# Convolution and involution over 32 images: patches for the 7x7 taps stored in DRAM plane by plane

## The chip, the core and the metric

The kernel runs on one core of a Trainium2 chip. The metric is the device time of one execution in microseconds; the number for a kernel is the median of its runs. The engines of the core are TensorE (PE; its weight loads are shown as PEld), VectorE (DVE), ScalarE (ACT), GpSimd (POOL) and SyncE (SP). SP and ACT both issue DMAs, each on a queue of its own, and the 16 DMA engines of the core serve both queues.

## What is computed

The input is `x` of 32 images x 64 channels x 56 x 56, in float32. Two residual steps follow each other, each on a group norm with 32 groups of two channels. This is the reference, cut:

```python
# step 1: binary 3x3 convolution
xb, wb = jnp.sign(_gn(x)), jnp.sign(weight)
x = x + conv(xb, wb, padding=1) * scale
# step 2: involution, 7x7 taps, 16 groups of 4 channels
v = _gn(x)
r = relu(batchnorm(w_r @ v + b_reduce))          # 64 -> 16 channels
ker = (w_s @ r + b_span)                         # 16 -> 49 * 16 channels, one 7x7 kernel per pixel and group
for ki in range(7):
    for kj in range(7):
        out = out + vpad[:, :, :, ki:ki + H, kj:kj + W] * ker[:, :, ki * 7 + kj][:, :, None]
x = x + out
```

## The kernel before

Two images make a **pair**, whose 2 x 64 channels are the 128 partitions; there are 16 pairs. For each pair the kernel makes the convolution on PE and adds it on DVE (`chunks`), takes the statistics (`variance`, `root`, `affine`), and normalizes (`normalize`, ACT) into `xn`. Since the span weights are the same for every pixel, the involution is reordered: PE multiplies shifted patches of `v` with the span weights (`taps`), DVE multiplies the result with `r` (`product`, L792), POOL folds two halves (L365), and PE sums over the 16 channels of `r` (`sums`).

**Patches.** A patch matrix has taps and positions on the partitions and pixels on the free dimension. It stands in two stacks of 128 rows, `X1` (`patches`, three buffers) and `X2` (`patches2`, two buffers), each fp16. They are filled out of DRAM: PE transposes `xn` (`transposes`), ACT copies the result in fp16, the high part (`high`, L404), DVE takes the rest, the low part (`low`, L783), and SP writes both to `D` in DRAM (`parts_out`, L270), four pieces k of 256 KB in each of two DMAs a pair. ACT's `high` of piece k waits until piece k-2 has been written, since the two share a buffer.

A pair's image is cut into seven **strips** (I call them s = 0 to 6). A stack row group of 16 rows is a **plane**: a part (high or low) with a vertical offset. For every strip SP loads the eight planes of `X1` with eight DMAs of 16 rows (`first_stack`, L287), and two low planes of `X2` with two DMAs (`second_stack`, L295). Their rows are 32 to 95 in steps of 4, and 0 to 31 and 96 to 127 in steps of 2. The other five planes of `X2` are planes that `X1` has too; ACT copies them in SBUF, 96 rows by 1792 columns in each of four instructions (`copy_high`, L432). The selection matrices of `constants()` place each tap's weights on the rows where its plane stands.

**Order.** Every engine runs a program written out by hand. A strip has eight units n; unit n of all 56 of a pair is `taps` on PE, `product` on DVE, a fold on POOL. The tables at the top of the file (L75 to L86) say behind which unit of the current pair each piece of work for the next pair stands: the convolution at units 11 to 17 (strips 1 and 2), the statistics at 18 to 21 (strip 2), the transposes with `high` and `low` at 28, 30, 34, 36 (strips 3 and 4), the reduction with `relu` at 37 and 38 (strip 4). Of a strip's eight ACT steps, the four copies for the next strip stand at steps 0, 1, 4 and 5, `gather` of the strip before (osb from PSUM, then a DMA to `sums_dram`) at step 3, and `rows` at step 7, which waits for that DMA to land and then loads it into `U`. `arrange` (L454) reorders `U` at units 13 and 46.

SP's program for strip e is: the second stack of strip e+1 (it waits until strip e-1 has left PE), the first stack of strip e+2, in strip 2 the store of the pair before, in strip 3 pieces 0 and 1 of the next pair's parts and the load of x for the pair after, in strip 4 pieces 2 and 3 and `spread`, 16 small DMAs that distribute `r` (L305). PE begins a strip when both its stacks are in and its copies are made (L564 to L566):

```python
                if n % GP == 0:
                    pe.wait_ge(first_in[e % 3], FIRSTLOAD * (e // 3 + 1))
                    pe.wait_ge(second_in[e % 2], SECONDLOAD * (e // 2 + 1))
                    pe.wait_ge(copied, JX * (e + 1))
```

## Time and profile before

| what | value |
|---|---|
| time, three runs | median 1971.62 us (1965.9 to 1975.86) |
| the profiled execution's own time | 1978.51 us |
| its span in the trace | 1976.6 us |
| mean granted TensorE clock | 0.922 |
| busy share: PE, DVE, ACT, POOL | 82%, 70%, 53%, 51% |
| DMA, moved | 410.7 MB, mean 208 GB/s |

The profile page and the trace are of one execution. A busy share is an average over the whole span. The views used below are the page, the table of waits (which engine stood idle before which line, and what it was that ended the idle time), tables by windows of time, timelines of one engine, and the list of DMA issues with the median time from issue to landing. In a row, `L432` is line 432 of the kernel, `SPq` and `ACTq` are DMA issues on those queues, and a bracket at the end gives the idle time before it and what ended it.

### The profile page before, as it was taken

How to read it: one execution, taken by the hardware profiler on the slowest of the kernel's cores; microseconds unless marked ns; L12 is line 12 of the kernel's file. 1: busy time of each engine (PE TensorE's matmuls, PEld its weight loads, DVE VectorE, ACT ScalarE, POOL GpSimd, SP SyncE). 2: the span in 40 equal slices, each digit the busy share in tenths (PEclk: the TensorE clock that was granted, in tenths of full speed). 3: DMA queues.
4: the chain of work that ended last, by engine and by line, in shares of the span. 5: the costliest groups of instructions: out<-in, count | busy, mean ns of one | idle time of the engine just before them, and what ended most of it. 6: DMA issues, size and time to landing. Idle time of an engine off the chain costs nothing.

```text
span 1976.6 us, 39046 instructions
## 1 busy us (share of the span) xinstructions
PE 1621.0 (82%) x15072; PEld 730.2 (37%) x15072; DVE 1378.6 (70%) x1699; ACT 1052.8 (53%) x758; POOL 1015.0 (51%) x904
## 2 busy tenths in 40 slices
PE   3488897978889797896978878798887988889885
PEld 1233443434333343343433334333333433334332
DVE  5476776858768685776867767586776767768674
ACT  2255555545655554555545655465555545655562
POOL 1145555554645555455554645555455554645673
PEclk8799998999999998998989989898989999989997
DMA  4679899797998969899798998979799797998993
GB/s 106 158 168 237 185 238 224 199 233 172 245 216 217 236 173 239 186 244 215 188 240 181 250 215 205 230 183 247 175 240 225 187 250 180 248 215 205 227 243 85
DMA packets 215178, 410.70 MB, mean 208 GB/s; under 512 B 87406, under 2 KB 134815, under 8 KB 210847
## 3 DMA queue, kind: packets, MB, share of 16 engines
q1 hardware_dynamic: 139728, 356.81, 74.2%
q10 hardware_dynamic: 75264, 51.39, 10.1%
q8 instruction: 119, 1.95, 0.5%
q14 instruction: 67, 0.55, 0.1%
HBM read 310.30 MB, written 84.93 MB: 200 GB/s over the span
## 4 chain that ended last, share of the span: by engine, by line
POOL 46%; issue 42%; SPq 4%; DMA 2%; DVE 2%; PE 2%; ACT 1%; POOLq 1%; ACTq 0%; DVEq 0%
POOL folded L365 46%; SPq L305 2%; DMA patches<-parts_dram 1%; SPq L287 1%; PE ybank L571 1%; DMA back<-consts_dram 1%; POOLq L364 0%; SPq L257 0%; ACT patches L432 0%; DVE prod L792 0%; SPq L295 0%; PE ybank L541 0%; DMA parts_dram<-parts 0%; DVE parts L783 0%; SPq L270 0%
## 5 line engine op out<-in xcount | busy, mean ns | idle before, releaser
L365 POOL TENSOR_TENSOR folded<-prod 128x448 f32<-128x448 f32 x896 | 1009.3, 1139 | 941.3 <-DVE prod L792 940.0
L792 DVE TENSOR_TENSOR prod<-ybank,relu 128x896 f32<-128x896 f32 x896 | 961.1, 1088 | 406.9 <-PE ybank L571 333.4
L571 PE MATMUL ybank<-patches,wspan 128*64 128x448 f16 x7168 | 863.7, 382 | 240.2 <-DMA patches<-parts_dram 110.4
L432 ACT ACTIVATE patches<-patches 96x1792 f16<-96x1792 f16 x448 | 736.8, 1689 | 589.8 <-DMA patches<-parts_dram 306.9
L571 PEld LDWEIGHTS ybank<-patches,wspan 128*64 128x64 f16 x7168 | 396.3, 116 | 757.6 <-issue 416.1
L512 PE MATMUL ybank<-sgn,convw 128*128 128x448 bf16 x1008 | 205.6, 357 | 24.5 <-ACT sgn L385 20.1
L589 PE MATMUL obank<-folded,esum 128*32 128x448 f32 x1792 | 214.8, 551 | 1.5 <-POOL folded L365 1.5
L582 PE MATMUL obank<-patches,wbias 128*32 128x448 f16 x3584 | 197.8, 364 | 0.0
L512 PEld LDWEIGHTS ybank<-sgn,convw 128*128 128x128 bf16 x1008 | 93.4, 97 | 137.8 <-issue 33.5
L582 PEld LDWEIGHTS obank<-patches,wbias 128*32 128x32 f16 x3584 | 87.4, 99 | 105.2 <-issue 52.7
L783 DVE TENSOR_TENSOR parts<-ybank,parts 128x1024 f16<-128x1024 f32 x64 | 78.5, 1226 | 60.5 <-ACT parts L404 60.5
L750 DVE SCALAR_TENSOR_TENSOR xs<-ybank,scale,xs 128x896 f32<-128x896 f32 x64 | 66.0, 1032 | 73.7 <-PE ybank L512 73.6
L404 ACT ACTIVATE parts<-ybank 128x1024 f16<-128x1024 f32 x64 | 65.3, 1020 | 68.1 <-PE ybank L541 64.5
L603 PE MATMUL ybank<-back,blocks 128*128 128x128 f32 (+1 forms) x448 | 62.2, 284 | 44.2 <-DVE prod L792 36.0
L541 PE MATMUL ybank<-ident,xn 128*128 128x128 f32 x512 | 74.3, 293 | 20.9 <-DVE parts L783 20.1
L420 ACT ACTIVATE osb<-obank,alpha 128x448 f32<-128x448 f32 x112 | 69.3, 619 | 29.7 <-PE obank L589 29.7
L603 PEld LDWEIGHTS ybank<-back,blocks 128*128 128x128 f32 (+1 forms) x448 | 48.2, 153 | 77.7 <-DVE prod L792 52.2
L541 PEld LDWEIGHTS ybank<-ident,xn 128*128 128x128 f32 x512 | 59.4, 148 | 44.4 <-DVE parts L783 25.5
L454 ACT ACTIVATE blocks<-rows 128x1792 f32<-128x1792 f32 (+1 forms) x32 | 54.1, 1690 | 40.0 <-DMA relu<-blocks 31.9
L754 DVE BATCH_NORM_STATS2 bn<-xs 128x6 f32<-128x448 f32 x112 | 70.2, 627 | 3.9
L804 DVE TENSOR_TENSOR xs<-ybank,xs 128x1024 f32<-128x1024 f32 (+1 forms) x64 | 61.8, 966 | 12.8 <-PE ybank L603 12.7
L734 DVE TENSOR_REDUCE rowsums<-xs 128x14 f32<-128x784 f32 x64 | 61.1, 959 | 12.5 <-DMA xs<-x_dram 12.5
(90 smaller groups left out, 380.0 us busy)
## 6 DMA issues: line engine op xcount, KB each, us to landing
patches<-parts_dram SPq DMA_DIRECT2D x1120, 224.0 KB, 7.0
parts_dram<-parts SPq DMA_DIRECT2D x128, 256.0 KB, 7.7
xs<-x_dram SPq DMA_DIRECT2D x128, 196.0 KB, 5.0
sums_dram<-osb ACTq DMA_DIRECT2D x112, 224.0 KB, 6.2
rows<-sums_dram ACTq DMA_DIRECT2D x112, 224.0 KB, 6.6
out_dram<-xs SPq DMA_DIRECT2D x128, 196.0 KB, 3.7
relu<-blocks SPq DMA_DIRECT2D x256, 49.0 KB
patches<-gb_dram SPq DMA_DIRECT2D x1, 784.0 KB
```

What stands on the lines that cost most here:

```text
L365: pool.tensor_tensor(folded[:, u % 8, :], prod[:, u % 2, 0, :], prod[:, u % 2, 1, :], ALU.add).then_inc(fold_done, 1)
L420: act.activation(osb[:], Obank[e % 2][:, 0:N], ACT.Copy, scale=alpha[:]).then_inc(o_read, 1)
L432: act.activation(X2[0:COPIED_ROWS, e % 2, at], X1[0:COPIED_ROWS, e % 3, at], ACT.Copy).then_inc(copied, 1)
L512: mm = pe.matmul(bank("conv", p, k)[:, i, 0:CW], convw[:, tap, :], sgn[:, CR * row + dh:CR * row + dh + CR, dw:dw + W], start=(tap == 0), ...
L541: mm = pe.transpose(bank("t", p, k)[:, y, 128 * h:128 * h + 128], xn[:, COLS * cy:COLS * cy + COLS], ident[:])
L571: mm = pe.matmul(bank("unit", p, n)[64 * t:64 * t + 64, h, 0:N], wspan[:, stack, g, h, :], of_group(e, stack, g), start=(stack == 0), stop ...
L582: pe.matmul(Obank[e % 2][32 * t:32 * t + 32, 0:N], wbias[:, stack, g, :], of_group(e, stack, g), start=(stack == 0 and i == 0), stop=False)
L589: mm = pe.matmul(Obank[e % 2][32 * (gp // 2):32 * (gp // 2) + 32, 0:N], esum[:, 16 - 16 * (gp % 2):48 - 16 * (gp % 2)], folded[:, 4 * half ...
L603: mm = pe.transpose(bank("out", p, k)[:, i, rows * n:rows * (n + 1)], V[0:rows, by].rearrange("m b g c -> m (b g c)"), back[0:rows, group, ...
L754: link(dve.bn_stats(bn[:, row, :], at[:, i, :]))
L783: dve.tensor_tensor(at(1), bank("t", p, k)[:], at(0), ALU.subtract).then_inc(low_done, 1)
L792: dve.tensor_tensor(prod[:, u % 2].rearrange("m h (n c) -> m h n c", c=GC), bank("unit", p, n)[:, :, 0:N].rearrange("m h (n c) -> m h n c" ...
```

## The change

- `D` is replaced by two DRAM tensors. `D0` holds for each of 128 source rows the eight planes of `X1`, each in a run of 2048 elements that is already shifted by the plane's offset. `D1` holds the two low planes of `X2`. A part that several planes need is written once for each: `parts_out` issues ten DMAs for piece 0 and six for each of the others, where it issued two, and writes 10 planes where there were 4 half images (5.0 MB a pair where it was 2.1 MB).
- The first stack of a strip is one DMA of 128 partitions, on SP. The rows of the stack are now 8 r + q, for row r of plane q.
- ACT copies all 128 rows of the first stack to the second, at steps 0, 1, 2 and 3 of a strip. It then waits for its own copies and issues two DMAs, on its own queue, that load the two low planes over rows 3, 11, ... and 7, 15, ... of `X2`. `gather` moves from step 3 to step 4.
- The load and the store of a pair's x are one DMA of 128 partitions each, where they were eight of 16.

```diff
-COPIED_ROWS, COPIED_PLANES = 96, 5
+PLANES = (((0, 0), (0, 2), (0, 4), (1, 1), (0, 1), (0, 3), (1, 0), (1, 2)),
+          ((0, 0), (0, 2), (0, 4), (1, 3), (0, 1), (0, 3), None, (1, 4)))
+Q = 8
+
+LOADED = (3, 7)
...
-XLOAD, STORE = 16 * 8, 16 * 8
-FIRSTLOAD, SECONDLOAD = 16 * 8, 16 * 2
+XLOAD, STORE = 16, 16
+FIRSTLOAD, SECONDLOAD = 16, 16 * 2
 COPY = JY * 128
-DWRITE = 16 * 2
+DWRITE = (16 * 10, 16 * 6)
...
-SUMS_B, BIAS, SUMS_A, ROWS_AT = 3, 6, 7, 7
-
-COPY_AT = {0: 0, 1: 1, 4: 2, 5: 3}
+SUMS_B, GATHER, BIAS, SUMS_A, ROWS_AT = 3, 4, 6, 7, 7
+
+COPY_AT = {0: 0, 1: 1, 2: 2, 3: 3}
...
             def load(p):
-                for rows in ROWS16:
-                    sp.dma_start(xs[rows, p % 3, :], xv[p][rows]).then_inc(x_loaded, 16)
+                sp.dma_start(xs[:, p % 3, :], xv[p]).then_inc(x_loaded, 16)
...
-                for l in range(2):
-                    sp.dma_start(D[p % 2, l].rearrange("m (y h n) -> m y h n", y=2, h=4)[:, :, k, :],
-                                 Ev[:, l, k % 2]).then_inc(d_written[k], 16)
+                b = p % 2
+
+                def run(dram, planes, q, l, y, shift, many):
+
+                    src = Ev[:, l, k % 2, y]
+                    if k == 0:
+                        for i in range(many):
+                            cut = BLOCK * (shift + i)
+                            sp.dma_start(dram[b, :, q + i, 0:4 * BLOCK - cut], src[:, cut:]).then_inc(d_written[k], 16)
+                        return
+                    dst = bass.AP(tensor=dram.tensor, offset=(128 * b * planes + q) * RUN + BLOCK * (4 * k - shift),
+                                  ap=[[planes * RUN, 128], [RUN - BLOCK, many], [1, 4 * BLOCK]])
+                    sp.dma_start(dst, src.unsqueeze(1).broadcast_to((128, many, 4 * BLOCK))).then_inc(d_written[k], 16)
+
+                run(D0, Q, 0, 0, 0, 0, 3)
+                run(D0, Q, 4, 0, 1, 0, 2)
+                run(D0, Q, 6, 1, 0, 0, 2)
+                run(D0, Q, 3, 1, 1, 0, 1)
+                run(D1, 2, 0, 1, 1, 1, 1)
+                run(D1, 2, 1, 1, 0, 2, 1)
...
-                for l, a, row, step in PLANES[0]:
-                    sp.dma_start(X1[row:row + 15 * step + 1:step, e % 3, :],
-                                 plane(e, l, a)).then_inc(first_in[e % 3], 16)
...
+                sp.dma_start(X1[:, e % 3, :].rearrange("p (j n) -> p j n", j=JX), stack(D0, e)).then_inc(first_in[e % 3], 16)
...
-                act.activation(X2[0:COPIED_ROWS, e % 2, at], X1[0:COPIED_ROWS, e % 3, at],
-                               ACT.Copy).then_inc(copied, 1)
+                act.activation(X2[:, e % 2, at], X1[:, e % 3, at], ACT.Copy).then_inc(copied, 1)
+
+            def second_stack(e):
+
+                act.wait_ge(copied, JX * (e + 1))
+                if e >= 2:
+                    act.wait_ge(second_in[e % 2], SECONDLOAD * (e // 2))
+                p = e // E
+                for i, q in enumerate(LOADED):
+                    src = bass.AP(tensor=D1.tensor, offset=(2 * (128 * (p % 2) + 4 * JX * (e % E)) + i) * RUN,
+                                  ap=[[2 * RUN, 16], [8 * RUN, JX], [1, JY * 128]])
+                    act.dma_start(X2[q:128:Q, e % 2, :].rearrange("p (j n) -> p j n", j=JX), src).then_inc(second_in[e % 2], 16)
```

The first place to look at is ACT, from `normalize` in strip 2 through strip 3 to strip 4. A row is an instruction with what it writes and reads; `parts` is `high`, `osb` and `sums_dram` are `gather`, `patches2` are the copies. Before:

```order
L396 ACTIVATE xn<-xs,small 128x28x56 x2
L445 DMA rows<-sums_dram 32x16x112
L432 ACTIVATE patches2<-patches 96x1792 x2
L420 ACTIVATE osb<-obank0,alpha 128x448
L424 DMA sums_dram<-osb 128x448
L404 ACTIVATE parts<-ybank2 128x1024
L432 ACTIVATE patches2<-patches 96x1792 x2
L404 ACTIVATE parts<-ybank2 128x1024
L445 DMA rows<-sums_dram 32x16x112
L432 ACTIVATE patches2<-patches 96x1792 x2
L404 ACTIVATE parts<-ybank1 128x1024
```

The same stretch of ACT in the changed kernel:

```order
L399 ACTIVATE xn<-xs,small 128x28x56 x2
L458 DMA rows<-sums_dram 32x16x112
L435 ACTIVATE patches2<-patches 128x1792 x4
L446 DMA patches2<-planes2_dram 16x4x1792 x2
L407 ACTIVATE parts<-ybank2 128x1024
L423 ACTIVATE osb<-obank0,alpha 128x448
L427 DMA sums_dram<-osb 128x448
L407 ACTIVATE parts<-ybank2 128x1024
L458 DMA rows<-sums_dram 32x16x112
L435 ACTIVATE patches2<-patches 128x1792 x2
L407 ACTIVATE parts<-ybank1 128x1024
```

In strip 3 all four copies and the two DMAs of the second stack now stand ahead of the first `high`, where two copies and `gather` stood; in strip 4 `high` still stands behind two copies.

The second place is SP from strip 3 to strip 5, before: `parts_dram` are the pieces, `xs` the load of x, `relu` is `spread`.

```order
L270 DMA parts_dram<-parts 256x1x512 x4
L257 DMA xs<-x_dram 16x3136 x8
L295 DMA patches<-parts_dram 16x4x1792 x2
L287 DMA patches<-parts_dram 16x4x1792 x8
L270 DMA parts_dram<-parts 256x1x512 x4
L305 DMA relu<-blocks 16x1x784 x16
L295 DMA patches<-parts_dram 16x4x1792 x2
L287 DMA patches<-parts_dram 16x4x1792 x8
```

The same place in the changed kernel, from the end of piece 1 of the next pair's parts:

```order
L281 DMA planes_dram<-parts 128x512 x3
L257 DMA xs<-x_dram 128x3136
L302 DMA patches<-planes_dram 128x4x1792
L281 DMA planes_dram<-parts 128x3x512
L281 DMA planes_dram<-parts 128x2x512 x2
L281 DMA planes_dram<-parts 128x512 x3
L281 DMA planes_dram<-parts 128x3x512
L281 DMA planes_dram<-parts 128x2x512 x2
L281 DMA planes_dram<-parts 128x512 x3
L311 DMA relu<-blocks 16x1x784 x16
L302 DMA patches<-planes_dram 128x4x1792 x5
```

The second stack no longer stands behind the 16 DMAs of `spread`; the first stack still does, and pieces 2 and 3 are 12 issues ahead of `spread` where they were four.

## Rows read from the trace of the kernel before

**Rows 1.** The page: busy time of the engines, and the two DMA queues.

```profile
PE 1621.0 (82%) x15072; PEld 730.2 (37%) x15072; DVE 1378.6 (70%) x1699; ACT 1052.8 (53%) x758; POOL 1015.0 (51%) x904
...
q1 hardware_dynamic: 139728, 356.81, 74.2%
q10 hardware_dynamic: 75264, 51.39, 10.1%
```

**Rows 2.** The table of waits: us in total, times, longest us.

```profile
ACT patches L432 <- DMA patches<-parts_dram: 306.9, 45, 13.1
...
PE ybank L571 <- DMA patches<-parts_dram: 110.4, 15, 9.1
PE ybank L571 <- ACT patches L432: 91.5, 29, 20.0
```

**Rows 3.** Windows, DVE's products alone: stretch, us, DVE busy, PEclk, DMA share, GB/s.

```profile
923.50:937.40 13.90, 8.64 (x9) 0.94 0.96 214
937.40:958.70 21.30, 8.51 (x9) 1.00 0.55 135
958.70:975.30 16.60, 8.59 (x9) 1.00 0.82 206
975.30:988.20 12.90, 8.61 (x10) 1.00 0.99 252
988.20:1007.10 18.90, 8.63 (x10) 0.91 1.05 262
1007.10:1024.90 17.80, 8.61 (x9) 0.89 0.82 226
1024.90:1041.40 16.50, 8.60 (x8) 0.91 1.04 232
```

**Rows 4.** Windows: us, busy PE PEld DVE ACT POOL, PEclk, DMA share, GB/s.

```profile
2.50:3.10 0.60, 0.00 (x0) 0.00 (x0) 0.00 (x0) 0.00 (x0) 0.60 (x1) 1.00 0.92 363
...
4.00:11.00 7.00, 0.00 (x0) 0.00 (x0) 0.00 (x0) 1.35 (x2) 2.22 (x3) 1.00 0.99 216
...
57.60:68.00 10.40, 5.59 (x46) 1.96 (x44) 3.67 (x3) 4.67 (x5) 0.00 (x0) 0.97 0.60 202
...
77.40:79.00 1.60, 0.00 (x0) 0.00 (x0) 0.00 (x0) 0.32 (x1) 0.00 (x0) 0.50 1.01 201
...
988.20:1007.10 18.90, 16.37 (x158) 6.23 (x158) 10.92 (x12) 11.12 (x9) 9.88 (x9) 0.91 1.05 262
```

**Rows 5.** Timeline of SP's issues: start, us, line, what is moved, count.

```profile
7.29 0.36 SPq L316 DMA_DIRECT2D patches<-gb_dram  x1
...
1001.18 2.55 SPq L270 DMA_DIRECT2D parts_dram<-parts  x4
1005.52 12.81 SPq L305 DMA_DIRECT2D relu<-blocks  x16
1018.43 1.26 SPq L295 DMA_DIRECT2D patches<-parts_dram  x2
```

**Rows 6.** Timeline of PE, the first units of strip 6 of this pair.

```profile
1023.15 4.67 PE L571 MATMUL ybank<-patches,wspan 128*64 128x448 f16 x24 [7.09 <-DMA patches<-parts_dram]
```

**Rows 7.** Timeline of ACT in strips 2 and 3 of this pair.

```profile
966.36 0.20 ACT L390 ACTIVATE small<-small 128x1 f32<-128x1 f32 x1 [6.95 <-DVE small L767]
...
975.49 3.26 ACT L432 ACTIVATE patches<-patches 96x1792 f16<-96x1792 f16 x2
978.65 0.61 ACT L420 ACTIVATE osb<-obank,alpha 128x448 f32<-128x448 f32 x1
...
980.26 1.02 ACT L404 ACTIVATE parts<-ybank 128x1024 f16<-128x1024 f32 x1 [0.99 <-PE ybank L541]
```

**Rows 8.** DMA issues: count, KB each, median us from issue to landing.

```profile
patches<-parts_dram SPq DMA_DIRECT2D x1120, 224.0 KB, 7.0
...
sums_dram<-osb ACTq DMA_DIRECT2D x112, 224.0 KB, 6.2
...
patches<-params_dram SPq DMA_DIRECT2D x1, 331.5 KB, 2.9
```

50 lines of the change are left out of this document (22 added, 28 removed), and 3 rows, old and new, of the table PLANES.

## The prediction

> **What bounds the kernel now.** I read the waits first, then the strips, then the DMA rates. No engine is busy all the time: PE has 82% of the span [rows 1]. PE stands 110.4 us, in 15 waits of about 7.4 us, for patches out of DRAM, and 91.5 us in 29 waits for ACT's copies; ACT itself waits 306.9 us for the first stack ahead of its copies [rows 2]. So about 202 us of PE's idle time, 12.6 a pair, go back to patches that are late.
>
> The windows of [rows 3] are the seven strips of one pair (117.9 us), each cut at DVE's first product of a strip (x8 complete products in each; a further count is one that is cut). Strips 0, 1 and 3 (13.9, 21.3, 12.9 us) are set by engines: DVE and PE have their work back to back there. Strips 4, 5 and 6 (18.9, 17.8, 16.5 us) lie at a DMA share of 1.05, 0.82 and 1.04. Of strip 5's 17.8 us, 7.1 are one stall of PE ahead of strip 6 [rows 6]; 10.7 are left. TensorE's granted clock is 1.00 in strips 1 to 3 and 0.89 to 0.94 in those with stalls [rows 3]; I count nothing for what fewer stalls would give back there. Its cause stands in [rows 5]: SP issues `spread` from 1005.52 for 12.81 us, and only at 1018.43 the second stack that PE waits for. That is the wait that comes 15 times.
>
> The DMA side: q1 is busy 74.2% of 1976.6 us, 91.7 us a pair, and q10 10.1%, 12.5 us [rows 1]: 104 of about 118 us. The queues are near full, so what a transfer costs in DMA time counts.
>
> **DMA time, part by part.** A rate below is GB/s over the DMA share, what the 16 engines would move if all were busy. One load into 128 partitions (the parameters) runs at 363/0.92 = 395. The last two planes of a first stack, whose rows are 96 to 127 in steps of 2, run at 201/1.01 = 199. The load of x in 16-row DMAs runs at 216/0.99 = 218, the parts into DRAM at 202/0.60 = 337 [all rows 4].
>
> - First and second stack, before: 70 DMAs of 224 KB [rows 8] are 16.1 MB a pair. Of q1's 91.7 us, x takes 3.2 MB / 218 = 14.7, the parts 2.1 MB / 337 = 6.2, `spread` 0.8 MB some 3; 68 are left, a mean rate of 237.
> - First stack after: 12.8 MB in 128-partition DMAs. Bounds: 199 (64 us) and 395 (32 us). I take 343, 37 us, nearer to the 395, because that row has the same shape of destination, with a deduction for long reads beside other traffic.
> - Second stack after: 3.2 MB in rows 8 apart, 16 rows again. I take the 199 of the step of 2: 16 us. Upper bound of the rate 395: 8 us. Patches in all 53 where they were 68: -15.
> - x: 3.2 MB at 343 is 9.4: -5. The parts grow by 2.9 MB, at 337 +9 (at 199 +14).
>
> Sum -11, 93 us a pair, with ends at about -26 (all at 395, writes at 337) and +27 (both stacks and the added writes at 199, x as before).
>
> The Trainium skill, "DMA: Bandwidth & Descriptors", section The descriptor swizzle, says that a 128-partition transfer has each engine write through one SBUF port of its own, and that four neighbouring partitions share a port. 
>
> **The chain of a strip after the change.** The second stack now follows the copies. From the moment strip e-1 has left PE: four copies, 2 x 3.26 = 6.5 us [rows 7]; 0.2 for the wait on them; two issues on ACT, 1.26 us if they cost what SP's do [rows 5]; landing of the second. The nearest rows for that are 2.9 us (331.5 KB, empty queues) and 7.0 (loaded) [rows 8]; with the first stack of strip e+2 done by then, I take 3.5 after the issue starts. That is 6.5 + 0.2 + 0.6 + 3.5 = 10.8 us, 14.3 if loaded. PE needs it a strip later, so the chain hides in a strip of 12.9 us or more, if ACT starts on time. ACT's own round is 6.5 + 0.2 + 1.26 + 0.61 for `osb` and up to 1.0 around its DMA [rows 7], then `rows` waits 2.9 to 6.2 us for the sums to land [rows 8]: 12.5 to 15.8. It can fall behind by 2 to 3 us in a short strip and makes that good in strip 1. The copy of 128 rows rather than 96 I cost at nothing, as each lane copies the same 1792 columns.
>
> **Strip by strip**, now and then:
> - 0: 13.9, and 13.9. 1: 21.3, and 21.3. Engine work, unchanged.
> - 2: 16.6 and 16.6. ACT waits 6.95 us for `root` [rows 7]; one copy and the second stack are now behind it. `root` is over 966.6 - 958.7 = 7.9 us into the strip, so 1.6 + 0.2 + 0.6 + 3.5 later, at 13.8, the stack is in: inside the strip.
> - 3: 12.9 and 15.3. `high` stood at 980.26, behind two copies. It now stands behind four copies and two issues: 975.49 + 6.5 + 0.2 + 1.3 = 983.5, 3.2 later. DVE's `low` waits for it, and its products behind that; the 1 us or so that the second `low` waited before is recovered. I take +2.4 (bounds 0 and 3.2).
> - 4: 18.9 and 16. The first stack is in when the copies want it. Left are PE's 16.4 us of work [rows 4]. The buffer of `high` now waits for ten DMAs of piece 0, 6.4 us of issues at 0.64 each [rows 5], or 3.6 at 0.36; they end about as it is wanted.
> - 5: 17.8 and 13.2. The stall of 7.1 is gone (10.7 are left); the chain and a late `rows` put 2.5 back.
> - 6: 16.5 and 16.0. Its copies need a first stack that is still behind `spread`: pieces 2 and 3 are eight issues more, 3 to 5 us, and the earlier queue is shorter by as much. It lands 4 to 5 us into the strip, and the copies and the second stack follow, +10.8.
>
> That is 112.3 for 117.9, **-5.6 a pair**. Over 14 pairs -78. The first pair gets about -3; the last has nothing on the queues that waits, 0. At the start 28 issues for the parts stand where there were 8: at 0.36 to 0.64 each +7 to +13 us, less the 5 us of the seven issues fewer of the first stack, +5. Sum -76. Against the profiled execution: 1976.6 - 76 + 1.9 around the span = 1902.5, and the profile was 6.9 above the median of its runs (1978.51 against 1971.62), so **1895 us**.
>
> **Rivals.**
> - A, *the serial chain is the bound*. The second stack is loaded behind the copies on a queue that shares its DMA engines with the first stack. If it lands in 7.0 us and the sums in 6.2, the round is 15.8 and the chain 14.3: strips 0, 3, 5, 6 cost 1.5, 1, 2, 2 more than forecast. -5.6 + 6.5 = +0.9 a pair: about 1985; half of it, 1940. Against it: the DMA engines have more room. The same page of the Trainium skill, section Rules for kernel authors, says that spreading DMAs over issuing engines gives no bandwidth. That speaks for A wherever both stacks are under way together, and does not change its price.
> - B, *slower: DMA time grows*. The kernel writes 2.9 MB a pair more; that is paid only if the first stack is moved faster. DMA time stays as it is where the first stack's 12.8 MB take 48 us, a rate of 267, and the stall of 7.1 us won in strip 5 is used up as well at 55 us, 233. If it runs at about the mean rate before, 228, it takes 56: 56 + 16 - 68 + 9 = +13 (x no faster either), less 7.1, is +6 a pair while the queues stay as full as now: 1972 + 90 = 2060. For it: the same bytes come back out of DRAM, out of rows that lie as close. Against: the 395 of a 128-partition load.
> - C, *queues that empty*. The first stack at 395, `low` not held up in strip 3 (12.9), strips 4 and 6 at 15 and 14: 107 a pair, -150, about 1820.
> - D, the transfers are faster but nobody waits for them: ruled out by the 202 us of [rows 2], save as a part of A.
>
> **How the numbers follow.** Forecast, 1845 to 1940: 0.66. A: 0.15, of which a third is under 1962, a third within 0.5%. B: 0.07. C: 0.12. The forecast's own ends are the strip bounds (strip 3 between 0 and 3.2, strips 5 and 6 by 1.5 each way, 14 pairs) and the start. For 8 in 10 the range takes part of A and of C: 1835 to 1965. 0.5%, about what a measurement here can tell from no change, is 10 us: faster 0.66 + 0.12 + 0.05 = 0.83, same 0.05, slower 0.12.
>
> **What would show it.** Right: PE's 15 waits of 7.4 us before strip 6 gone; ACT's wait for the first stack well under 306.9; the DMA share in strips 3, 4 and 6 under 1; a first-stack DMA of 1792 KB landing in 6 to 8 us; a new idle time of about 2 us of DVE before the first `low` of a pair. Wrong: PE waiting for `planes2_dram` in most strips (A); windows at share 1 all through with less than 250 GB/s (B). The forecast fails most easily in the landing time of the second stack and in strip 6.

## The result: slower by 8%, and where the time went

The changed kernel has a median of 2133.5 us in four runs (2122.6 to 2134.4). The kernel before, run beside it, has 1970.3 (1965.9 to 1975.9 in four). The ratio is 1.081, with a 95% interval of 1.077 to 1.086. The forecast was 1895 us, range 1835 to 1965: it has the wrong sign. The profiled execution took 2133.4 us, its span is 2131.5, the mean granted clock 0.898.

From the page, to be set beside [rows 1]:

```profile
PE 1648.5 (77%) x15072; PEld 738.8 (35%) x15072; DVE 1379.1 (65%) x1699; ACT 1055.7 (50%) x758; POOL 1014.5 (48%) x904
...
q1 hardware_dynamic: 159952, 351.51, 47.9%
q10 hardware_dynamic: 93184, 102.79, 16.8%
```

The engines have the same work. The DMA queues moved 46 MB more, and were busy 64.7% of the span instead of 84.3%. That is 1379 us where it was 1666. This half of the change did what it should, and more.

The transfers are idle because they now wait, as the table of waits (total us, times, longest) shows. Beside it stand [rows 2].

```profile
PE ybank L587 <- DMA patches<-planes_dram: 259.9, 45, 31.7
...
DVE parts L799 <- ACT parts L407: 118.8, 52, 5.7
ACT blocks L467 <- DMA relu<-blocks: 116.8, 15, 9.1
ACT patches L435 <- DMA sums_dram<-osb: 115.2, 22, 8.8
ACT patches L435 <- DMA patches<-planes_dram: 107.1, 26, 13.3
```

ACT's wait for the first stack fell from 306.9 to 107.1 us, as intended. PE's wait for patches out of DRAM rose from 110.4 to 259.9. Three waits that [rows 2] did not name have grown: DVE's `low` for ACT's `high` (60.5 us before), ACT's `arrange` for `spread` (31.9), and ACT's `rows`, with the copies behind it, for the landing of the sums (68.3). In these rows both stacks are called `patches`, and both DRAM tensors `planes_dram`.

The seven strips of one pair, cut as [rows 3] and read by DVE's products alone (us, DVE busy, clock, DMA share, GB/s):

```profile
1386.70:1400.50 13.80, 8.59 (x8) 0.87 0.40 119
1400.50:1421.90 21.40, 8.61 (x10) 1.00 0.40 122
1421.90:1439.00 17.10, 8.57 (x9) 0.90 0.58 224
1439.00:1456.00 17.00, 8.57 (x9) 0.90 0.72 234
1456.00:1473.30 17.30, 8.49 (x9) 1.00 0.97 318
1473.30:1488.30 15.00, 8.62 (x8) 0.92 0.90 290
1488.30:1512.50 24.20, 8.62 (x8) 0.85 0.79 274
```

Strips 0 and 1 run at a DMA share of 0.40. The loss stands in strip 3 and, above all, in strip 6. Since one pair may be odd, I cut pairs 1 to 14 of every trace in the same way, at each strip's first product, and took the median of each strip over the 14 pairs. These medians are used below:

| strip | 0 | 1 | 2 | 3 | 4 | 5 | 6 | sum |
|---|---|---|---|---|---|---|---|---|
| before | 13.8 | 21.3 | 17.4 | 12.8 | 17.4 | 17.8 | 17.0 | 117.5 |
| forecast after | 13.9 | 21.3 | 16.6 | 15.3 | 16.0 | 13.2 | 16.0 | 112.3 |
| after | 13.8 | 21.3 | 17.4 | 17.0 | 17.5 | 14.9 | 24.9 | 126.8 |

By the medians a pair is 9.3 us longer. Medians hide that in three of the 14 pairs strip 0 lasts about 22 us instead of 13.8, so the sum goes by all 14 pairs: they are longer by 139.5 us, of which strip 6 has 100.5, strip 3 53.2 and strip 0 23.8, while strip 5 gives 43.8 back. The way to the first strip is 9.6 us longer, and the first and the last pair 2.9 each. Together that is 154.9, the difference of the spans.

**Strip 6, link by link.** First SP (start, us, line, what is moved, count). Strip 5 of this pair begins at 1473.3, strip 6 at 1488.3.

```profile
1455.40 4.26 SPq L281 DMA_DIRECT2D planes_dram<-parts  x6
1459.77 0.40 SPq L257 DMA_DIRECT2D xs<-x_dram  x1
1460.38 0.37 SPq L302 DMA_DIRECT2D patches<-planes_dram  x1
1460.85 15.07 SPq L281 DMA_DIRECT2D planes_dram<-parts  x12
1476.02 11.87 SPq L311 DMA_DIRECT2D relu<-blocks  x16
1488.12 12.94 SPq L302 DMA_DIRECT2D patches<-planes_dram  x3
```

The 12 issues of pieces 2 and 3 take 15.07 us, 1.26 each (15.7 for the twelve by the median of the 14 pairs); the six of piece 1, just before, take 4.26, 0.71 each. The same timeline cut to two of the twelve shows where it sits:

```profile
1462.04 7.86 SPq L281 DMA_DIRECT2D planes_dram<-parts  x2
```

One of these two is of the usual 0.6 us, the other holds SP for 7.2; the remaining ten lie at 0.4 to 1.3. It stands behind the load of x (1.6 MB) and a first stack (1.8 MB), which were issued just before it. This pair has the longest such issue of the 14; in the others the longest of the twelve takes 2.5 to 5.9 us. Then comes `spread`, and behind it the first stack for strip 0 of the next pair. It goes out at 1488.12. It needs not only the buffer that strip 4 has left at about 1473, but also all four pieces in DRAM, and the last of them lands at 1482.50; so `spread` ahead of it costs at most 5.6 us, and the pieces themselves the rest. It lands 7.4 us into strip 6. There ACT and PE take over (timelines of ACT, PE and SP, with the idle time ahead of a row and what ended it in brackets):

```profile
1495.65 6.46 ACT L435 ACTIVATE patches<-patches 128x1792 f16<-128x1792 f16 x4 [3.78 <-DMA patches<-planes_dram]
1502.14 1.19 ACTq L446 DMA_DIRECT2D patches<-planes_dram  x2
```

```profile
1499.72 0.95 PE L587 MATMUL ybank<-patches,wspan 128*64 128x448 f16 x8
...
1510.79 4.69 PE L587 MATMUL ybank<-patches,wspan 128*64 128x448 f16 x24 [9.23 <-DMA patches<-planes_dram]
```

```profile
1500.71 0.36 SPq L302 DMA_DIRECT2D patches<-planes_dram  x1
```

So: landed 7.4 us into the strip, copies 6.46, two issues, and PE starts 8.6 us after the first of them, 22.5 us into a strip that took 17.0 us before. That last 8.6 us is a transfer of 448 KB beside another first stack, which SP issues at 1500.71, when PE has done the last unit of strip 6 (1499.72 + 0.95) and so left its buffer.

The 14 pairs show the price of this neighbour. In 11 of them SP issues that first stack between 1.8 us ahead of the second stack and 0.2 us behind it, and the second stack takes 8.0 to 9.1 us to land. In the other three SP issues it 1.2 to 1.5 us later, and the second stack lands in 4.2 to 5.4; strip 6 then takes only 20.4 to 22.6 us. The three pairs that follow are those with the long strip 0: there a first stack is issued up to 1.5 us ahead of the second stack for strip 1, which takes 8.3 to 9.1 us instead of 4.2. The loss has moved by one strip.

Strip 5 has a chain of its own: PE stands 4.2 us (median) ahead of strip 6 in all 14 pairs, for the second stack. The first stack for strip 6 is the one issued at 1460.38, behind x. By the median over the pairs such a stack lands 14.6 us after its issue, where those for strips 4 and 0 take 7.2 and 7.5.

**Strip 3, the queue on ACT.** The timelines of ACT and of DVE at the turn of strips 3 and 4:

```profile
1440.45 6.46 ACT L435 ACTIVATE patches<-patches 128x1792 f16<-128x1792 f16 x4 [1.70 <-DMA sums_dram<-osb]
1446.94 1.21 ACTq L446 DMA_DIRECT2D patches<-planes_dram  x2
1448.26 1.02 ACT L407 ACTIVATE parts<-ybank 128x1024 f16<-128x1024 f32 x1 [1.34 <-issue]
```

```profile
1449.31 1.22 DVE L799 TENSOR_TENSOR parts<-ybank,parts 128x1024 f16<-128x1024 f32 x1 [4.36 <-ACT parts L407]
```

DVE stands 4.36 us, and its products stand behind `low`. This is the step forecast at "+2.4 (bounds 0 and 3.2)". By the median of the 14 pairs `high` starts 9.3 us into strip 3, where it was 5.1: the 4.2 us by which the strip is longer. The copies start 1.5 us into the strip (0.5 ahead of it before), as ACT's `rows` first waits for the sums; it goes out within 0.03 us of their landing in all 14 pairs. The copies take 6.5 us, and the two issues 1.3. The second stack for strip 4 plays no part here: it lands 3.6 us before PE wants it.

### The profile page after: what moved, and what is told of

Its sections match the earlier page's. It is cut to its first block, busy times and chain, and to the rows that moved or that the text cites. A ratio compares the mean times of both kernels' runs of the same rounds, so it can differ in the third digit from the quotient of the medians.

```text
span 2131.5 us, 38358 instructions
## 1 busy us (share of the span) xinstructions
PE 1648.5 (77%) x15072; PEld 738.8 (35%) x15072; DVE 1379.1 (65%) x1699; ACT 1055.7 (50%) x758; POOL 1014.5 (48%) x904
## 3 DMA queue, kind: packets, MB, share of 16 engines
q1 hardware_dynamic: 159952, 351.51, 47.9%
## 4 chain that ended last, share of the span: by engine, by line
issue 37%; POOL 33%; SPq 9%; DMA 5%; DVE 5%; PE 5%; ACT 5%; ACTq 1%; POOLq 0%; DVEq 0%
POOL folded L368 33%; SPq L281 5%; ACT patches L435 3%; SPq L311 3%; PE ybank L587 2%; DMA sums_dram<-osb 2%; DVE prod L808 1%; DMA patches<-planes_dram 1%; SPq L277 1%; ACTq L446 1%; DMA relu<-blocks 1%; DVE parts L799 1%; ACT parts L407 1%; PE obank L605 1%; DMA back<-consts_dram 1%
## 5 line engine op out<-in xcount | busy, mean ns | idle before, releaser
L587 PE MATMUL ybank<-patches,wspan 128*64 128x448 f16 x7168 | 879.6, 388 | 315.3 <-DMA patches<-planes_dram 259.9
L435 ACT ACTIVATE patches<-patches 128x1792 f16<-128x1792 f16 x448 | 726.0, 1685 | 453.7 <-PE ybank L587 231.3
L587 PEld LDWEIGHTS ybank<-patches,wspan 128*64 128x64 f16 x7168 | 402.9, 118 | 848.7 <-issue 503.3
L605 PE MATMUL obank<-folded,esum 128*32 128x448 f32 x1792 | 223.2, 571 | 1.5 <-POOL folded L368 1.5
L799 DVE TENSOR_TENSOR parts<-ybank,parts 128x1024 f16<-128x1024 f32 x64 | 78.3, 1224 | 119.5 <-ACT parts L407 118.8
L407 ACT ACTIVATE parts<-ybank 128x1024 f16<-128x1024 f32 x64 | 65.5, 1024 | 117.5 <-PE ybank L557 60.3
L467 ACT ACTIVATE blocks<-rows 128x1792 f32<-128x1792 f32 (+1 forms) x32 | 54.3, 1697 | 129.4 <-DMA relu<-blocks 116.8
L399 ACT ACTIVATE xn<-xs,small 128x1568 f32<-128x1568 f32 x32 | 58.9, 1898 | 27.9 <-DVE small L792 27.9
```

What stands on the lines that cost most here:

```text
L407: act.activation(Ev[:, 0, k % 2], bank("t", p, k)[:], ACT.Copy).then_inc(high_done, 1)
L435: act.activation(X2[:, e % 2, at], X1[:, e % 3, at], ACT.Copy).then_inc(copied, 1)
L587: mm = pe.matmul(bank("unit", p, n)[64 * t:64 * t + 64, h, 0:N], wspan[:, stack, g, h, :], of_group(e, stack, g), start=(stack == 0), stop ...
L605: mm = pe.matmul(Obank[e % 2][32 * (gp // 2):32 * (gp // 2) + 32, 0:N], esum[:, 16 - 16 * (gp % 2):48 - 16 * (gp % 2)], folded[:, 4 * half ...
L799: dve.tensor_tensor(at(1), bank("t", p, k)[:], at(0), ALU.subtract).then_inc(low_done, 1)
```

## The experiments

Two theories stood at the start. **Chain**: the second stack now has to follow the copies, and that series is what costs (rival A of the prediction). **Queue**: the time is lost in front of it, where SP issues the first stack late. The texts written before the runs call them theory S and theory Q. The first edits take each away.

### x loaded earlier on SP, alone

```diff
+                    if s == 3 and p + 2 < pairs:
+                        load(p + 2)            # now ahead of pieces 0 and 1
                     ...
-                    if s == 3 and p + 2 < pairs:
-                        load(p + 2)            # was behind them, ahead of the first stack
```

> The changed kernel with one edit: the load of x for the pair after next stands at the head of strip 3's work on SP, ahead of pieces 0 and 1, and no longer between them and the first stack of strip 4's turn. Theory Q (SP's queue in strips 4 and 5 makes the first stack for the next pair late; that alone makes strip 6 25 us long): the twelve issues of pieces 2 and 3 took 15.4 us since the ring was full of x and a first stack; they fall to 8 to 11 us, the first stack of strip 5 is issued 4 to 6 us earlier, strip 6 falls from 25 to 19 to 21 us, and the kernel to about 2133 - 15 x 5 = 2060 us. Theory S (the second stack behind the copies is what is late; the queue is full anyway): strip 6 stays at 24 to 25 us, 2120 to 2140 us.

Measured: 2076.9 us, 1.055 of before (1.049 to 1.060), so 56 us less than the changed kernel. SP's timeline of this kernel:

```profile
1418.73 11.72 SPq L281 DMA_DIRECT2D planes_dram<-parts  x12
1430.54 12.85 SPq L311 DMA_DIRECT2D relu<-blocks  x16
1443.62 14.27 SPq L302 DMA_DIRECT2D patches<-planes_dram  x3
```

The twelve issues take 11.7 us instead of 15.1 (medians of the 14 pairs 12.1 and 15.7): the load of x, when it is ahead of them, holds them up. Strip 6 fell all the same only from 24.9 to 24.0, against the 19 to 21 expected of theory Q. Most of the gain is in strip 5, 14.9 to 11.9 us, where the first stack for strip 6 no longer stands behind x and lands in 9.3 us instead of 14.6. The queue is a part of the loss, and not all of it: `spread`, 12.85 us, is still in front of the first stack, which leaves at 1443.62 when strip 5 ends.

### The same, and the first stack ahead of `spread`

```diff
-                            spread(p + 1)       # in strip 4, behind piece 3
+                        if s == 5:
+                            spread(p + 1)       # behind strip 5's first stack
```

> As the kernel with the early x, and also the first stack of strip 5 is issued ahead of spread (the 16 DMAs of r), which follows it. Theory Q: the stack goes out at the start of strip 5, some 12 us before it did; ACT's copies in strip 6 wait for nothing, but arrange and the step behind it end 3 to 5 us later than they did relative to the start of strip 5. Strip 6 falls to 17 to 18 us, the kernel to 2133 - 15 x 7.5 = 2020 us (1990 to 2040). Theory S: with the stack early, strip 6 is still over 22 us and the kernel over 2090.

Measured: 2070.5 us, 1.051 (1.048 to 1.055), 6 us less than the run before, which is within the spread of both. Strip 6 is down to 17.7 us, and strip 5 up from 11.9 to 16.5: the sum of the two, 34.2, is hardly less than the 35.9 of the run before. SP's timeline of one pair shows that the first stack now waits for the pieces: their issues end at 1418.80, and it goes out at 1424.07.

```profile
1408.63 10.17 SPq L281 DMA_DIRECT2D planes_dram<-parts  x12
1424.07 0.37 SPq L302 DMA_DIRECT2D patches<-planes_dram  x1
```

There it is the neighbour of the second stack for strip 6, which takes 9.1 us to land where it took 5.3 (medians), and PE stands for it in all 14 pairs. That is what strip 5 lost. The waits say what else came:

```profile
ACT blocks L468 <- DMA relu<-blocks: 189.3, 15, 14.7
...
PE ybank L620 <- ACT blocks L468: 44.4, 15, 7.5
```

L620 is `back`, the transposition for the outputs; it needs what `arrange` (L468) writes in strip 5, and `arrange` writes over the buffer `V` out of which `spread` reads, so that it waits for all 16 DMAs: now 189.3 us, where it was 98.1 in the run before. In strips 4 and 5 the pieces, `spread` and the first stack all want SP's queue, and each order makes another one late.

### The low planes of the second stack left out

```diff
             def second_stack(e):
-                act.wait_ge(copied, JX * (e + 1))
                 ...
-                    act.dma_start(X2[q:128:Q, e % 2, :]..., src).then_inc(second_in[e % 2], 16)
+                pass
...
-                    pe.wait_ge(second_in[e % 2], SECONDLOAD * (e // 2 + 1))
```

> The changed kernel without the two DMAs that load the low planes over the copy, and without the waits on them: this leaves out the part of the result that these two planes carry. ACT still copies all rows. It prices the serial step behind the copies. Theory Q: strip 6 loses the 7 to 8 us between the last copy and the landing (25 to 17 us), strips 3, 4 and 5 about 1 us each, in all 2133 - 15 x 10 = 1980 us, still not under the kernel before. Theory S: without the step nothing is late any more, strips 2 to 6 fall to 13 to 16 us, and the kernel to 1900 us or less.

Measured: 1906.2 us, 0.968 (0.963 to 0.972), 227 us under the changed kernel. That is the price of the serial step with all that hangs on it, and it turns the verdict round. It bounds the price from above, as the 448 KB a strip and ACT's two issues are left out with the wait. What is left of the loss can be seen in its strips 3, 5 and 6, and in its waits:

```profile
1285.70:1298.50 12.80, 8.44 (x9) 1.00 0.69 240
...
1314.20:1324.10 9.90, 8.63 (x8) 1.00 0.97 313
1324.10:1345.50 21.40, 8.53 (x8) 0.84 0.69 213
```

```profile
PE ybank L611 <- ACT blocks L460: 132.9, 16, 9.3
...
ACT blocks L460 <- DMA relu<-blocks: 147.7, 15, 11.2
```

Strip 3 is at its 12.8 us again, strip 5 at 9.9, and only strip 6 is long, by the late `spread`. By the medians it takes 22.5 us, of 24.9 in the changed kernel. So strip 6 is held by two paths of nearly the same length, the second stack and `spread` with what follows it, and taking one away shortens it little. The 227 us come from strips 5, 3 and 0 (5.1, 3.7 and 1.7 us a pair on the mean) before strip 6 (1.8). And strip 3's part is ACT's program, which has lost the two issues as well, rather than PE's wait for the load.

### No copies, the low planes loaded as they are

```diff
+                if e >= 2:
+                    at = slice(COPY * j, COPY * j + 8)     # 8 columns of each copy's 1792
                 act.activation(X2[:, e % 2, at], X1[:, e % 3, at], ACT.Copy).then_inc(copied, 1)
```

> The changed kernel where, after the first two strips, ACT copies 8 columns in each of its four copies in place of 1792: the shared planes of the second stack are left out, the two loads behind the copies stay. It splits the serial step: the chain loses 6.3 of its 6.5 us of copying and keeps the landing. Theory S1 (the landing under load, up to 8 us and not 3.5, is what hurts): it still has waits for the low planes in strips where the first stack and x are on the queue; about 1980 to 2020 us. Theory S2 (it is the length of the whole chain that hurts, either half short would hide it): as fast as the kernel without the loads, about 1900 us. Both leave strip 6 at 22 us, since SP is as late.

Measured: 1937.7 us, 0.981 (0.976 to 0.986). The second stack is still loaded, still behind a wait on the "copies", and 196 of the 227 us are back. So neither the load nor the wait is dear alone. It is the length of the series: copies of 6.5 us, then a load. With either half short, the rest hides in a strip. (ACT's own time falls too without the copies, 71 us of them where there were 726, so a part of the 196 us may be that.) Strip 6 stays at 23.5 us here as well.

### Planes that keep 96 rows apart, so that nothing follows the copies

The second stack's low planes lie in rows of their own here, as in the kernel before; the first stack is two DMAs, of 96 rows (6 r + q) and of 32, and the copies are of 96 rows. x is early too, and the first stack of strip 5 ahead of `spread`, as in the second experiment.

```diff
-FIRSTLOAD, SECONDLOAD = 16, 16 * 2
+FIRSTLOAD, SECONDLOAD = 16 * 2, 16
...
-                sp.dma_start(X1[:, e % 3, :]..., stack(D0, e)).then_inc(first_in[e % 3], 16)
+                for rows, dram, planes in ((slice(0, 96), D0, 6), (slice(96, 128), D1, 2)):
+                    sp.dma_start(X1[rows, e % 3, :]..., stack(dram, planes, e)).then_inc(first_in[e % 3], 16)
```

> A version between the two: planes written out in DRAM as in the change, x in one DMA and early, the first stack of strip 5 ahead of spread; but the six planes of the first stack that the second shares or may overwrite lie in rows 0 to 95 (6 r + q) and come as one DMA of 96 partitions, two more in rows 96 to 127 as one DMA of 32; ACT copies 96 rows at steps 0, 1, 4, 5 as before, gather at step 3, and the two low planes of the second stack are one DMA of 32 rows on SP that waits for no copy. Theory Q: both costs of the change are gone and the faster stack stays: strips about 13.8, 21.3, 16.8, 12.9, 16, 13, 16 us, 110 a pair, about 1850 us (1820 to 1890). Rival: a stack of 96 and 32 rows is no faster than one of 16-row DMAs, the queues are full and it comes out at 1950 or more.

Measured: 2100.5 us, 1.066 (1.064 to 1.069). From its page, the list of issues (count, KB, median us to landing), and the waits:

```profile
q1 hardware_dynamic: 177872, 402.90, 75.6%
...
patches<-planes_dram SPq DMA_DIRECT2D x112, 1344.0 KB, 11.1
```

```profile
ACT blocks L469 <- DMA relu<-blocks: 262.2, 15, 19.9
...
PE ybank L618 <- ACT blocks L469: 234.3, 17, 17.0
```

1344 KB now need 11.1 us, where 1792 KB in 128 partitions need 9.3, as a row in the section on what was right shows. The chain is gone, strip 3 is at 12.8, and PE waits only 5.9 us in all for patches out of DRAM. But the gain in DMA time is gone with it: both queues are busy 85.2% of the span, as before the change. And strip 6 takes 29.0 us, since PE stands 234.3 us for `arrange`, behind the late `spread`; strip 4 takes 22.2. So this run shows that the gain in DMA time went when the 128 rows were split in 96 and 32. It does not show what such a layout costs in time, as it also has `spread` behind the first stack, an order that costs 70 us where the low planes are left out (below). The split layout with `spread` in its old place was not run.

### The chain cut in two halves

As the second experiment, with each low plane loaded in two parts, behind copies 2 and 4.

```diff
-            def second_stack(e):
-                act.wait_ge(copied, JX * (e + 1))
+            def second_stack(e, half):
+                act.wait_ge(copied, JX * e + 2 * (half + 1))
```

> The changed kernel with early x, the first stack of strip 5 ahead of spread, and the second stack loaded in two halves: after two copies the low planes of the first two columns blocks, after all four the rest (four DMAs of 112 KB for two of 224 KB). The last landing covers half the bytes. Theory S1: landing under load falls by 1 to 3 us, 1.2 us more issues on ACT are against it: 2070 - 15 x 2 = 2040 us, 2010 to 2070.

Measured: 2140.7 us, 1.084 (1.077 to 1.091), 70 us more than without the halves. Strips 3 and 6 are longer by 1.5 and 1.8 us, strip 4 is 0.5 shorter, and in five of the 14 pairs strip 0 takes 20.4 to 22.3 us and the pair 134 or more. Whatever the overlap gives, it is less than what four issues on ACT instead of two bring with them; which of these is the cause was not isolated.

### The low planes left out, and x early; then also the stack ahead of `spread`

> The changed kernel without the loads of the two low planes (their part of the result is left out) and with the early x. In the kernel without the loads alone, PE waited 133 us, in strip 6, for arrange, which waits for spread, and the first stack of strip 5 came late as well; both stand behind pieces 2 and 3 on SP. If that is right, the early x shortens the issues of pieces 2 and 3 from 15.6 to about 11 us, strip 6 from 22.5 to 18, and the time from 1906 to 1840 to 1860 us. If strip 6 stays at 22, the wait for arrange has another cause.

> As the one before, and the first stack of strip 5 ahead of spread (the low planes are left out here too). The stack can no longer be late, but spread starts some 2 to 4 us later, so that arrange and the outputs at unit 50 wait longer. If spread is what binds strip 6 now: the same as with the early x alone or up to 30 us slower. If the stack is: 20 to 40 us faster.

Measured: 1873.1 us, 0.949 (0.942 to 0.956), and 1943.4, 0.985 (0.979 to 0.991). With the chain away, x early still gives 33 us. But putting `spread` behind the first stack now costs 70, where with the chain there it changed nothing that can be told from the spread of the runs. The wait of ACT in the two kernels, for `spread`:

```profile
ACT blocks L461 <- DMA relu<-blocks: 224.6, 15, 16.0
```

and it is 139.4 us in the first of the two. The chain of `spread`, `arrange` and outputs is thus a bound of its own, right beside the patches: strip 6 takes 20.0 us in the first of the two and 25.6 in the second. The prediction has no line for it.

### The second stack on SP, in time with the copies

```diff
+            def second_stack(e):                # on sp: ahead of piece 0 in strip 3,
+                sp.wait_ge(copied, JX * (e + 1))   # between pieces 2 and 3 in strip 4,
                 ...                             # between the halves of spread in strip 5
-                            spread(p + 1)
+                            spread(p + 1, (0,))
+                        if s == 5:
+                            second_stack(e + 1)
+                            spread(p + 1, (1,))
```

> The changed kernel with the early x, and the two DMAs behind the copies issued by SP and no longer by ACT (in strips 3 and 4 between the pieces, in strip 5 between two halves of spread). All work is done. ACT loses the wait on its copies and 1.2 us of issues a strip, and high, gather and normalize stand no longer behind them; the sums no longer queue behind 448 KB. If ACT's turn is what the serial step costs: strips 3, 4 and 5 fall by 2 to 3 us each, 2077 - 15 x 6 = 1985 us. If it is the landing behind the copies alone: no change, 2060 to 2090 us.

x is early here as well. Measured: 2040.1 us, 1.034 (1.027 to 1.041), 93 under the changed kernel, of which x early alone gives 56, with all work done. Its waits:

```profile
ACT blocks L474 <- DMA relu<-blocks: 234.2, 15, 18.0
PE ybank L591 <- DMA patches<-planes_dram: 234.0, 56, 26.1
```

ACT's queue is free of the issues, and strip 6 is at 17.5 us; `spread` is now the late one (234 us). Strip 5 has risen to 18.8 us, since PE stands 8.0 us ahead of strip 6 for the second stack, and strip 3 keeps 15.8 where it was 12.8.

### The second stack behind `gather` on ACT; then with x early

```diff
-                        if COPY_AT[n % GP] == JX - 1:
-                            second_stack(e + 1)
+                    if n % GP == GATHER and e + 1 < EALL:      # right behind osb and its DMA
+                        second_stack(e + 1)
```

> The changed kernel with one edit: ACT issues the two DMAs of the second stack behind gather and, in strips 3 and 4, behind high, and no longer ahead of them. All work is done. If high and the sums behind these DMAs are a main part of the cost, strips 3 and 4 fall by 1 to 2 us each: 2133 - 15 x 3 = 2090 us. If the landing of the low planes is, it comes 1.5 to 2.5 us later in every strip and the time is 2133 to 2190 us.

> The changed kernel with both edits that helped alone: the early x (-56 us) and the two DMAs of the second stack behind gather and high on ACT (-60 us). All work is done. If they are separate costs, they add up: 2133 - 116 = 2017 us (2000 to 2030). If both bought the same slack in strip 6, it stays at 2060 or more.

Measured: 2072.8 us, 1.050 (1.045 to 1.054), and 2048.8, 1.038 (1.034 to 1.042). The order on ACT alone is worth 61 us. Of the waits of the first of the two:

```profile
DVE parts L799 <- ACT parts L407: 52.0, 51, 5.5
...
ACT patches L435 <- DMA sums_dram<-osb: 28.1, 4, 7.7
```

Both fell, from 118.8 and 115.2: with the sums sent first they land in time for `rows`, and ACT enters the next strip in time. Strip 3 went from 17.0 to 13.8 us, but strip 4 from 17.5 to 20.3: the second stack now goes out later, and PE stands 3.5 us for it ahead of strip 5. Over the 14 pairs strip 3 gives 37.7 us and strip 4 takes 30.1 back; the gain that is left is in strip 0 (23.8, the three long ones are gone), in strip 5 (18.1) and in the last pair (13.6).

The two edits together give 85 us, where each alone gives 61 and 56, 32 less than the sum. One reason can be read off: with both, strip 3 is at 16.1 again. `high` is early (5.5 us into the strip), but the second stack for strip 4 now has x beside it, and PE stands 3.3 us for it where it stood 1.3.

### `spread` on POOL's queue, in the changed kernel and in the one before

What is left on SP in strips 4 to 6 is `spread`. Here POOL issues it, four DMAs in each of units 40 to 43.

```diff
+                if u // UNITS + 1 < pairs and 40 <= u % UNITS < 44:
+                    spread(u // UNITS + 1, u % UNITS - 40)      # pool.dma_start, 4 of the 16
```

> As the one before, and spread is issued by GpSimd, four DMAs in each of units 40 to 43, and no longer by SP (16 DMAs, 11.7 us of SP's time). All work is done. If spread on SP's queue is what is left in strip 6, the first stack of strip 5 goes out 12 us earlier and arrange waits less: strip 6 falls from about 23 to 15 to 17 us, less 2 to 4 us that GpSimd's issues cost in strip 5: 1920 to 1950 us, under the kernel before. If the wait for r or ACT's order is what binds, strip 6 stays over 20 us and the time over 1990.

Measured: 2024.8 us, 1.027 (1.023 to 1.031). That is 24 us less than the run before, not the 100 and more that I expected. The price of issuing on POOL shows on DVE, which waits for the folds to free its buffers: 42.5 us in the run before, and here

```profile
DVE prod L812 <- POOL folded L372: 153.2, 196, 3.9
```

Strip 6 did fall, from 23.9 to 16.3 us, as expected; strip 5, in which POOL issues, rose from 13.1 to 17.7.

### The small part of the change alone: x in one DMA

In the kernel before, only the load and the store of x become one DMA of 128 partitions each.

```diff
-XLOAD, STORE = 16 * 8, 16 * 8
+XLOAD, STORE = 16, 16
...
-                for rows in ROWS16:
-                    sp.dma_start(xs[rows, p % 3, :], xv[p][rows]).then_inc(x_loaded, 16)
+                sp.dma_start(xs[:, p % 3, :], xv[p]).then_inc(x_loaded, 16)
```

> The kernel before with one part of the change alone: x is loaded and stored as one DMA of 128 partitions. Its packets take 0.47 us where they took 0.69 and more, and SP has 14 issues fewer a pair (9 us). Both theories: DMA time falls by about 4 us a pair out of 104, which comes back in strips 4 to 6; 1970 - 16 x 2 to 4 = 1905 to 1940 us.

> As the kernel before with x in one DMA, and also spread is issued behind the second stack in strip 5 and no longer ahead of it. The 15 stalls of 7.4 us of PE ahead of strip 6 should go, but the first experiments showed a step that I had not priced: spread must land before arrange, and arrange before the outputs at unit 50 of the pair. Expected: stall down from 7.1 to about 2 us, some of it back at unit 50; 1870 to 1910 us.

Measured: 1941.8 us, 0.983 (0.980 to 0.987), and, with `spread` moved behind the second stack as well, 1943.6, 0.983 (0.979 to 0.987). The first is the one part of the change that was seen to pay by itself, 32 us under the kernel before beside it (1974.0). The second is the test of the prediction's first reading, that PE's 15 waits of 7.4 us ahead of strip 6 are there to be won. These waits are gone, strip 5 fell from 17.5 to 12.2 us, and nothing was gained: strip 6 rose from 17.4 to 22.8. Its waits:

```profile
PE ybank L570 <- ACT patches L431: 180.7, 48, 20.9
```

With x in one DMA alone this wait was 105.3 us. PE went on to strip 6 in time and then stood for strip 0's copies, whose first stack was as late as ever. The first stall had only hidden the next one.

Last, x in one DMA and `spread` on POOL's queue, in the kernel before:

> The kernel before with x in one DMA (1942 us) and spread issued by GpSimd in the same way. The 15 stalls of 6.8 us ahead of strip 6 have to go if their cause is spread on SP ahead of the second stack, and now nothing else is pushed behind it: 1942 - 15 x 5 = 1865 us (1850 to 1890). If the full DMA queues are the cause, the stalls shrink by 2 us at most: 1910 to 1940.

Measured: 1926.5 us, 0.977 (0.972 to 0.982). It is the fastest kernel here that does all the work, 2.3% under the one before, and still 36 us above the upper end of what I expected of it. The time lies in the range of the other theory, 1910 to 1940, but not by its mechanism: the stalls of PE ahead of strip 6 have not shrunk by 2 us, they are gone. Strip 5 has yet stayed at 17.4 us (17.5 without the edit). The page (line 355 is POOL's issue: count, busy us, mean ns) and the waits say why:

```profile
L355 POOL DMA_DIRECT2D relu<-blocks x256 | 144.0, 600 | 60.0 <-ACT blocks L414 57.4
```

```profile
DVE prod L794 <- POOL folded L367: 172.6, 210, 4.5
DVE prod L794 <- PE ybank L573: 171.3, 134, 26.1
```

The sixteen issues take POOL 9 us a pair, all in strip 5, and DVE waits 8.9 us a pair for POOL there: one stall has been put in the place of another.

## Why the prediction was wrong, point by point

**Right: the DMA time.** The forecast took 343 GB/s for the first stack, between bounds of 199 and 395. A window of the changed kernel in which there is hardly anything but first stacks on the engines (two, issued at 970.07 and 970.66; us, busy PE PEld DVE ACT POOL, clock, DMA share, GB/s), and the list of issues:

```profile
974.00:977.00 3.00, 2.99 (x14) 2.08 (x16) 1.01 (x1) 0.00 (x0) 0.18 (x1) 0.50 1.00 400
```

```profile
patches<-planes_dram SPq DMA_DIRECT2D x112, 1792.0 KB, 9.3
...
patches<-planes_dram ACTq DMA_DIRECT2D x224, 224.0 KB, 3.8
```

400 GB/s, the upper bound. The sum of DMA time, forecast 104 to 93 us a pair, came out at 1379 / 16 = 86. Landing took 9.3 us where "6 to 8" stood, as the median holds those that wait behind x (14.6 us, for strip 6) or behind another first stack (13.4, for strip 1); those for strips 0 and 4 took 7.5 and 7.2. The Trainium skill, "DMA: Bandwidth & Descriptors", section The descriptor swizzle, has each engine write one port of its own in a 128-partition transfer. The prediction read a full rate out of that, and the 400 agrees.

**Right: strips 0 and 1**, as engine work, but for the three long strips 0; **strip 2** had 17.4 both before and after (I took one pair's 16.6). PE's stall ahead of strip 6 is gone as it stood, and strip 5 is shorter by 2.9 us, of the 4.6 forecast.

**Wrong, the largest: strip 6**, "It lands 4 to 5 us into the strip, and the copies and the second stack follow, +10.8", 16.0 us; measured 24.9. This is the step that fails the forecast. Three terms of it were off, all in one direction.
- "pieces 2 and 3 are eight issues more, 3 to 5 us": the twelve take 15.1 us where four took 2.6 [rows 5], so 12.5 more. I priced an issue by the time it takes when the queue has room. Behind 3.4 MB of x and a first stack, one issue took 7.2 us. By the run with x early 3.4 us of the 15.1 are x's (15.07 against 11.72).
- The first stack landed at 7.4 us (median 8.1) and not at 4 to 5. It left only when strip 6 began and then took its 7.5 us. "The earlier queue is shorter by as much" did not hold: SP was 12.5 us longer at pieces 2 and 3.
- "I take 3.5 after the issue starts": a single one lands in 3.8 by the median of all strips, but here the two took 8.6, because PE leaves strip 6 just as ACT has made the copies, and that sets another first stack free. The condition that I gave for the 3.5, "with the first stack of strip e+2 done by then", fails just where the chain is critical. The loaded value of 7.0, which I held as the bound, was still too low: 8.0 to 9.1 in 11 of 14 pairs.

7.4 + 6.5 + 8.6 = 22.5 us, in a strip that was forecast at 16. Before the change the four copies took the same 6.5 us [rows 7], but nothing followed. Nor would the right price of this chain alone have given the strip: without the second stack it still takes 22.5 us, for `spread` (below), which the same 12.5 us on SP have made late.

**Wrong: strip 3**, +2.4 forecast, +4.2 measured (12.8 to 17.0); strip 4, 16 forecast, 17.5 measured; strip 5, 13.2 forecast, 14.9. In strip 3 "975.49 + 6.5 + 0.2 + 1.3" took the order of ACT rightly, and took for given that ACT starts on time. It doesn't: its copies start 1.5 us into the strip, behind `rows`, which waits for the sums, and the change puts their DMA behind the copies and the issues of the second stack. So the sentence that ACT "makes that good in strip 1" was not enough: it is behind again by strip 3. The run with the sums ahead of the second stack shows it, with 13.8 us for strip 3, though the second stack that it makes later takes most of that back in strip 4. The two issues cost what was forecast: ACT stands 1.34 us in all from the copies to `high`.

**Missing: `spread`, `arrange`, outputs.** The prediction followed SP's queue to its next user, the first stack, and not to the users of what it moved. ACT waits 116.8 us for `spread` in the changed kernel, and where the chain is away, the place of `spread` alone is worth the 70 us between the two runs without low planes. It holds strip 6 at 22.5 us without the second stack and at 23.5 without the copies.

**The rivals.** The mechanism of A, the serial chain, is the one that came nearest: without the series the same kernel is 0.968 of before. It is not the whole of it, as SP's long issues, ACT's order and `spread` stand beside it. I gave it 0.15 and the price of 1985, because I added its excess strip by strip (1.5 + 1 + 2 + 2) with landing times out of rows in which no first stack starts at the same moment. B, that DMA time grows, is refuted by 64.7%. C was right in what it needed of the DMAs (the 395) and wrong in that this makes the kernel fast. Chance 0.83 for faster rested on the view that "near full" queues are what bounds the kernel; they were full, but what ended the waits was which transfer stood ahead of which.

**The first step.** "About 202 us of PE's idle time go back to patches that are late" counted waits as if each could be won alone. The run that removes the waits behind the 110 us gains nothing.

**Open.** The prices do not add up to one split: low planes out 227, copies out 196, order on ACT 61, x early 56, both 85, second stack on SP with x early 93. With `spread` on POOL's queue 2.7% remain. Its strip 3, 16.1 us for 12.8, is mostly the second stack for strip 4, for which PE stands 3.3 us in all 14 pairs, beside the early x: with x late strip 3 was 13.8. Why the issues of SP block behind megabytes, and how many may be under way before one does, no run tells.

## What to carry to other kernels

A transfer that becomes faster is worth what it takes off the last wait. If the layout that makes it fast puts a load behind a copy, the series of the two has to fit, with its landing time taken beside the largest transfer that can start at the same moment, into the shortest strip. An issue on a queue cost 0.4 to 0.7 us here when there was room and up to 7.2 behind megabytes: for each DMA added, count what stands ahead of it, and follow what it delays to the users of every transfer behind it, not just the next. And before a large rearrangement is judged, its small independent parts are worth a run of their own: one DMA for x gave 1.7%.

## What the runs showed of the hardware that I had not expected

- An issue can block: pieces that cost SP 0.71 us each on the mean took 15.1 us for twelve behind 3.4 MB that had just been issued, 11.7 with 1.6 MB of it moved away.
- The 448 KB of a second stack land in 4.2 to 5.4 us beside no first stack, or one issued over 1 us later, and in 8.0 to 9.1 when a first stack of 1792 KB was issued up to 1.8 us ahead of it, on another queue.
- A split into a 96-row and a 32-row DMA loses the gain of 128 rows. Over its busy time q1 moved 253 GB/s (402.9 MB in 75.6% of 2102 us), 249 with 16-row stacks (x in one DMA in both), and 344 with 128 rows (351.5 MB in 47.9% of 2131 us).
- Sixteen DMAs issued by POOL take it 9 us (600 ns each), and its folds come later for it, though a fold is no longer (1145 ns, 1139 before): DVE's waits for them rose from 42.5 us to 153.2, and from 41.0 to 172.6 in the kernel before with x in one DMA.
